# A transformer block with experts: order sums moved to accumulating transfers, a layer norm's statistics to ScalarE

## The reference, cut to what matters

```python
h = layernorm(x) * (1 + ca) + sa
x = x + ga * attention(h)        # x: (8, 1024, 256)
h = layernorm(x) * (1 + cb) + sb
x = x + gb * experts(h)

def attention(x):                # 16 heads of 16, orders n = 0..10, weight beta[n]
    q, k, v = x @ W_in.T, split into heads; xq, xk = clip(q / 4), clip(k / 4)
    Tq, Tk = chebyshev(xq), chebyshev(xk)
    num = sum_n Tq[n] * beta[n] * cumsum(Tk[n] * v)
    den = sum_n sum(Tq[n]) * beta[n] * cumsum(sum(Tk[n]))
    return (num / (den + 1e-7)) @ W_out.T

def experts(x):                  # 8 routed experts, 2 chosen, and one shared
    a = sqrt(softplus(x @ routing_W.T + bias)); top-2 of a give the weights
    return shared(x) + sum_e weight[e] * (silu(x @ W1[e] + b1[e]) @ W2[e] + b2[e])
```

## Time and profile before

| what | value |
|---|---|
| median of three runs | 1087.46 us (1085.91 to 1087.97) |
| the profiled execution | 1086.55 us |
| its span | 1084.9 us |
| PE busy | 948.9 us, 87% |
| DVE busy | 947.9 us, 87% |
| ACT busy | 472.5 us, 44% |
| POOL busy | 516.6 us, 48% |
| mean granted PE clock | 0.952 of full speed |

### The profile page before, as it was taken

The page is one execution under the profiler, slowest core; times in us unless marked ns, Lnnn a source line. Parts: engine busy times, 40 slices in busy tenths (PEclk is TensorE's granted clock), DMA queues, the critical chain, the costliest instruction groups (busy, mean ns, idle before and its releaser), DMA issues.

```text
span 1084.9 us, 15500 instructions
## 1 busy us (share of the span) xinstructions
PE 948.9 (87%) x4889; PEld 678.4 (63%) x4889; DVE 947.9 (87%) x1465; ACT 472.5 (44%) x702; POOL 516.6 (48%) x615
## 2 busy tenths in 40 slices
PE   3864749998998989999999999898999999889996
PEld 3643436675756666675757576675757576656774
DVE  1498989999999999999999999999999999999432
ACT  4334335372635445362635444362635445441431
POOL 2032646646645546536645546536645445454210
PEclk9876869999999999999999999999999999999999
DMA  8100001020202002020202011020202010020211
GB/s 270 45 1 20 20 0 50 1 59 1 69 1 59 1 9 60 0 58 0 69 0 58 0 16 53 0 58 0 69 0 39 0 24 25 1 39 1 44 21 20
DMA packets 31517, 34.18 MB, mean 32 GB/s; under 512 B 1299, under 2 KB 30430, under 8 KB 31462
## 3 DMA queue, kind: packets, MB, share of 16 engines
q1 hardware_dynamic: 21410, 22.72, 6.3%
q0 software_dynamic: 8448, 8.39, 5.9%
q10 hardware_dynamic: 1604, 2.46, 0.7%
HBM read 16.77 MB, written 16.79 MB: 31 GB/s over the span
## 4 chain that ended last, share of the span: by engine, by line
PE 32%; DVE 30%; issue 18%; POOL 11%; ACT 3%; DVEq 1%; POOLq 0%; ACTq 0%
PE ring L1257 13%; PE acc L1394 7%; DVE feat L945 7%; PE tr L1342 4%; PE tr L1310 4%; DVE feat L966 3%; POOL feat L625 2%; DVE hid L1094 2%; DVE feat L962 2%; DVE feat L1004 2%; DVE feat L1001 2%; POOL ms L357 1%; PE tr L1248 1%; DVE route L1083 1%; PE cfb L1368 1%
## 5 line engine op out<-in xcount | busy, mean ns | idle before, releaser
L784 ACT ACTIVATE hid<-ring,b1row 128x512 f32<-128x512 f32 x144 | 98.6, 685 | 163.5 <-PE ring L1257 163.5
L630 POOL TENSOR_TENSOR feat<-feat 128x1024 f32<-128x1024 f32 x32 | 75.6, 2364 | 197.7 <-DVE feat L962 152.8
L1394 PE MATMUL acc<-w,hid 128*128 128x256 f32 x640 | 156.6, 392 | 0.0
L1394 PEld LDWEIGHTS acc<-w,hid 128*128 128x128 f32 x640 | 117.1, 191 | 28.0 <-issue 14.5
L945 DVE TENSOR_TENSOR_SCAN feat<-zero,carry,feat 128x512 f32<-128x512 f32 x80 | 113.1, 1453 | 0.0
L945 DVE TENSOR_TENSOR_SCAN feat<-zero,feat 128x512 f32<-128x512 f32 x80 | 109.9, 1413 | 0.0
L1094 DVE TENSOR_TENSOR hid<-hid,cfb 128x512 f32<-128x512 f32 x128 | 86.2, 673 | 25.7 <-PE cfb L1368 25.3
L1257 PE MATMUL ring<-n2H,w1H 128*128 128x512 f32 x288 | 101.9, 436 | 0.0
L1257 PE MATMUL ring<-n1H,winH 128*128 128x512 f32 x192 | 67.3, 433 | 38.7 <-ACT hid L784 24.9
L742 ACT ACTIVATE feat<-ring,bqkv 128x512 f32<-128x512 f32 x96 | 65.7, 686 | 71.5 <-PE ring L1257 71.5
L382 ACT ACTIVATE ntok<-xin,ms 128x256 f32 (+1 forms) x64 | 33.2, 589 | 138.5 <-POOL ms L361 138.5
(11 more groups left out here) (169 smaller groups left out, 2238.7 us busy)
## 6 DMA issues: line engine op xcount, KB each, us to landing
xin<-in_L_attn_x SPq DMA_DIRECT2D x16, 512.0 KB, 5.5
out<-x SPq DMA_DIRECT2D x16, 512.0 KB, 4.5
out<-fin POOLq DMA_DIRECT2D x16, 512.0 KB, 6.2
gates<-gate_rows SPq DMA_DIRECT2D x16, 128.0 KB, 4.8
feat<-in_L_wmod SPq DMA_DIRECT2D x1, 1536.0 KB, 14.1
feat<-in_L_attn_W_in SPq DMA_DIRECT2D x1, 768.0 KB, 9.5
const<-in_constants ACTq DMA_DIRECT2D x1, 690.5 KB, 4.3
fin<-in_constants ACTq DMA_DIRECT2D x1, 512.0 KB, 5.2
```

The costliest lines, as they stand in the source:

```text
L630: g.tensor_tensor(f(W + 2 * n), f(W + 2 * n), f(W + 2 * n + 1), ALU.add).then_inc(added, 1)
L784: a.activation(hid[:, e % NG], ring[bank][:, :], ACT.Silu, bias=b1row[:, e:e + 1]).then_inc(ring_copied, 1)
L1394: last = mm(acc[t // 2][:, t % 2], x[:, t * P:(t + 1) * P], w[:, e // 2], start=False, stop=(e == E), skip_group_check=True)
```

## The change

- The second norm's statistics leave DVE. ACT takes the sum of each token with a Copy pass that also accumulates (`token_sums`), POOL makes minus the mean (`token_means`), ACT takes the sum of squared differences with a Square pass (`token_squares`, two halves), and POOL makes the scale and the shift with four operations (`inv_std_of_squares`). The passes' own output goes to an unused slot, `squared`, which is W+2.
- ACT's order: the sums stand before silu 2, the squares between the copies of k0, k1 and q0, `scale_even` behind `normalise_second`, `normalise_first` behind the high part of expert 6, the squares of the next chunk's keys between silu 6 and silu 7.
- `add_orders` becomes three accumulating transfers issued by POOL: W+1 to W, W+3 to W+4, then, when both have landed, W+4 to W. DVE's numerator keeps one add (W+2).
- DVE's order: the orders are scanned as 0, 1, 3, 4, 2; the scans of orders 3 and 4 stand right behind expert 3; the weighing of order 2, the first norm's statistics, the clips and the logit parts behind expert 4; the last numerator add before expert 8. The carry copies are merged from five to three.
- The softplus series is fitted anew with fewer terms: 10 operations instead of 13.

```diff
@@ -12,6 +12,7 @@
 K = 2
+LOG1P = (2.0000000076817583, 0.666663216413768, 0.40024595230747134, 0.2796515774481493, 0.2815777836368378)
...
@@ -148,6 +149,7 @@
         attn = feat[:, W + 1]
+        squared = feat[:, W + 2].rearrange("p h (a d) -> p (h a) d", a=NT // KD)
...
@@ -258,7 +263,7 @@
         ffn_gated = sem("ffn_gated")
-        NLOG, NSOFT, NCF, NSPLIT, NMV = 7, 13, 3, 7, 11
+        NLOG, NSOFT, NCF, NSPLIT, NMV = 7, 10, 3, 7, 11
@@ -373,6 +378,41 @@
+        def token_sums(act, i, p):
+
+            c = number(i, p)
+            for t in range(NT):
+                act.wait_ge(x1_ready, 2 * c + 1 + t // 2)
+                last = nc.scalar.activation(squared[:, t], x1[:, p, t], ACT.Copy, accum_out=ms[:, 1, 0, t:t + 1])
+            last.then_inc(sums_ready, 1)
+
+        def token_means(pool, i, p):
+
+            pool.wait_ge(sums_ready, number(i, p) + 1)
+            nc.gpsimd.tensor_tensor(ms[:, 1, 1], ms[:, 1, 0], k_("-1/D", NT), ALU.mult).then_inc(mean_ready, 1)
+
+        def token_squares(act, i, p, half):
+
+            act.wait_ge(mean_ready, number(i, p) + 1)
+            for t in (2 * half, 2 * half + 1):
+                last = nc.scalar.activation(squared[:, t], x1[:, p, t], ACT.Square, bias=ms[:, 1, 1, t:t + 1],
+                                            accum_out=ms[:, 1, 2, t:t + 1])
+            last.then_inc(squares_ready, 1)
+
+        def inv_std_of_squares(pool, i, p):
+
+            c = number(i, p)
+            at = 3 * c
+            t = lambda k: ms[:, 1, k]
+            pool.wait_ge(squares_ready, 2 * c + 2)
+            nc.gpsimd.tensor_tensor(t(3), t(2), k_("1/D", NT), ALU.mult).then_inc(var_steps, 1)
+            pool.wait_ge(var_steps, at + 1)
+            nc.gpsimd.tensor_tensor(t(4), t(3), k_("eps", NT), ALU.add).then_inc(var_steps, 1)
+            pool.wait_ge(var_steps, at + 2)
+            nc.gpsimd.tensor_tensor(t(9), t(4), k_("-half", NT), ALU.pow).then_inc(var_steps, 1)
+            pool.wait_ge(var_steps, at + 3)
+            nc.gpsimd.tensor_tensor(t(11), t(1), t(9), ALU.mult).then_inc(rstd_ready[1], 1)
+
...
@@ -621,13 +661,20 @@
                 pool.wait_ge(odd_ready, 4 * c + 2)
-                ge(pool, numerator, 2 * c)
+                ge(pool, numerator, c)
                 g.tensor_tensor(f(W + 4), f(KT5), f(V0), ALU.mult).then_inc(weighted5, 1)
             def add_orders(i, p, n):
-                pool.wait_ge(products, ND * number(i, p) + 2 * n + 2)
-                g.tensor_tensor(f(W + 2 * n), f(W + 2 * n), f(W + 2 * n + 1), ALU.add).then_inc(added, 1)
+                c = number(i, p)
+                if n < 2:
+                    pool.wait_ge(products, ND * c + 2 * n + 2)
+                else:
+                    pool.wait_ge(added[0], 16 * c + 16)
+                    pool.wait_ge(added[1], 16 * c + 16)
+                into, of = ((W, W + 1), (W + 4, W + 3), (W, W + 4))[n]
+                pool.sem_inc(sum_begun, 1)
+                g.dma_start(f(into), f(of), accum_op=ALU.add).then_inc(added[n], 16)
@@ -689,20 +736,22 @@
                 if st["second"]:
-                    inv_std(pool, 1, *later(i, p, -1))
+                    token_means(pool, *later(i, p, -1))
+                    inv_std_of_squares(pool, *later(i, p, -1))
                 if st["attn"]:
                     weigh_order_5(i, p)
                     if p == 0:
                         scale_wo(i)
                     add_orders(i, p, 0)
+                    add_orders(i, p, 1)
+                if st["second"]:
+                    exps(*later(i, p, -1))
+                if st["attn"]:
+                    add_orders(i, p, 2)
                 if st["norm"]:
                     inv_std(pool, 0, *later(i, p, 2))
                 if st["second"]:
-                    exps(*later(i, p, -1))
                     scores(*later(i, p, -1))
-                if st["attn"]:
-                    add_orders(i, p, 1)
-                if st["second"]:
@@ -750,8 +799,11 @@
                     act.wait_ge(clipped, 2 * c + q + 1)
+                    ge(act, summed, 2 * c - 1 + q)
                     if q == 0:
-                        ge(act, summed, 2 * c)
+                        ge(act, weighted, (ND - 1) * c)
+                        ge(act, weighted5, c)
+                    else:
@@ -830,13 +882,21 @@
                     highs(0, *nxt)
+                if second:
+                    token_sums(act, *prev)
                 silu(2)
-                if attn_:
-                    scale_even(i, p)
-                for half in HALVES[:4]:
-                    copy(half)
+                copy("k0")
+                if second:
+                    token_squares(act, *prev, 0)
+                copy("k1")
+                if second:
+                    token_squares(act, *prev, 1)
+                copy("q0")
+                copy("q1")
                 if second:
                     normalise_second(act, *prev)
+                if attn_:
+                    scale_even(i, p)
@@ -844,20 +904,22 @@
                     copy_logits(*prev)
-                if st["norm"]:
-                    normalise_first(act, *later(i, p, 2))
                 silu(5)
                 high(4)
                 copy("v0")
                 copy("v1")
                 silu(6)
+                if qkv:
+                    for which in range(3):
+                        square(*nxt, 0, which)
                 silu(7)
                 high(6)
+                if st["norm"]:
+                    normalise_first(act, *later(i, p, 2))
                 silu(8)
                 if qkv:
-                    for q in range(2):
-                        for which in range(3):
-                            square(*nxt, q, which)
+                    for which in range(3):
+                        square(*nxt, 1, which)
@@ -913,12 +975,15 @@
-            ORDERS = (0, 1, 3, 2, 4)
+            ORDERS = (0, 1, 3, 4, 2)
+
+            BY_WEIGHT = (0, 1, 3, 2)
+            NCARRY, CARRIED = 3, {0: 1, 1: 1, 3: 2, 4: 2, 2: 3}
             def weigh(i, p, j):
                 c = number(i, p)
-                n = ORDERS[j]
+                n = BY_WEIGHT[j]
@@ -929,6 +994,7 @@
                     dve.wait_ge(odd_ready, 4 * c + 1)
+                    ge(dve, squares_ready, 2 * c)
@@ -936,18 +1002,22 @@
                 if n < 4:
-                    dve.wait_ge(weighted, (ND - 1) * c + j + 1)
+                    dve.wait_ge(weighted, (ND - 1) * c + BY_WEIGHT.index(n) + 1)
                 else:
                     dve.wait_ge(weighted5, c + 1)
                 if p:
-                    dve.wait_ge(carried, ND * i + j + 1)
+                    dve.wait_ge(carried, NCARRY * i + CARRIED[n])
                 for h in range(KD):
                     last = v.tensor_tensor_scan(feat[:, W + n, h], zero[:, 0:1].to_broadcast([P, CT]), feat[:, W + n, h],
                                                 carry[:, n, h:h + 1] if p else 0.0, ALU.add, ALU.add)
                 last.then_inc(scanned, 1)
+
+            def carry_over(i, p, k):
+
                 if p == 0:
-                    dve.wait_ge(scanned, ND * c + j + 1)
-                    v.tensor_copy(carry[:, n], feat[:, W + n, :, CT - 1]).then_inc(carried, 1)
+                    at, n, j = ((0, 2, 1), (3, 2, 3), (2, 1, 4))[k]
+                    dve.wait_ge(scanned, ND * number(i, p) + j + 1)
+                    v.tensor_copy(carry[:, at:at + n], feat[:, W + at:W + at + n, :, CT - 1]).then_inc(carried, 1)
@@ -997,15 +1067,12 @@
                 dve.wait_ge(products, ND * c + ND)
-                dve.wait_ge(added, 2 * c + 1)
-                v.tensor_tensor(f(W), f(W), f(W + 4), ALU.add).then_inc(numerator, 1)
-                dve.wait_ge(numerator, 2 * c + 1)
-                dve.wait_ge(added, 2 * c + 2)
+                dve.wait_ge(added[2], 16 * c + 16)
                 v.tensor_tensor(f(W), f(W), f(W + 2), ALU.add).then_inc(numerator, 1)
             def divide(i, p):
                 c = number(i, p)
-                dve.wait_ge(numerator, 2 * c + 2)
+                dve.wait_ge(numerator, c + 1)
@@ -1060,18 +1127,16 @@
                 v.tensor_tensor(b(Z2), b(Z), b(Z), ALU.mult).then_inc(soft_steps, 1)
-                dve.wait_ge(soft_steps, at + 4)
-                v.tensor_scalar(b(PL), b(Z2), 2.0 / 15, 2.0 / 13, ALU.mult, ALU.add).then_inc(soft_steps, 1)
-                dve.wait_ge(soft_steps, at + 5)
-                v.tensor_tensor(b(PL), b(PL), b(Z2), ALU.mult).then_inc(soft_steps, 1)
-                for k, m in enumerate((11, 9, 7, 5, 3)):
-                    dve.wait_ge(soft_steps, at + 6 + k)
-                    v.scalar_tensor_tensor(out=b(PL), in0=b(PL), scalar=2.0 / m, in1=b(Z2),
+                v.scalar_tensor_tensor(out=b(PL), in0=b(Z), scalar=LOG1P[4], in1=b(Z),
+                                       op0=ALU.mult, op1=ALU.mult).then_inc(soft_steps, 1)
+                for k, m in enumerate((3, 2, 1)):
```

(58 more changed lines are left out.)

13 lines of the change are left out of this document (8 added, 5 removed).

## The result

| | before | changed |
|---|---|---|
| median | 1086.68 us, 4 runs | 1126.27 us, 4 runs (1125.12 to 1127.35) |
| ratio to before | | 1.0364, interval 1.0345 to 1.0383 |
| span of the profiled execution | 1084.9 us | 1123.3 us |

The account below looks back on a forecast made before the run. PE and DVE were both taken as critical early, DVE's run from expert 4 late. Thirteen steps at +0.8 (+10.4) and -4 at the edges gave +6.4 on 1086.55: 1093, adjusted to 1094; range 1066 to 1122.

Parts of the forecast that it names:

- what moves into the late stretch: DVE from expert 4 to the divide's end: 5.7 us in, one scan pair out, 24.5 us instead of 24.7.
- +0.8: Predicted growth of each of 13 full steps in us, from +0.9 in p=1 and +0.7 in p=0.
- The -4 of the edge steps: First two steps and the one before the last two, DVE-bound: two save 2 us each, together -4.
- the early stretch: Step up to expert 4: ScalarE passes and POOL's product delay `cfb` 4 to +32.45, expert 4 to +32.9 from +32.2.
- The 0.6 us for expert 8's weighing behind the last add: End of step: weighing after the numerator's last add makes PE start the out-projection at +57.9, after the divide at +57.3.
- Rival B: POOL's queue: transfers land late, at 9 us instead of 6.2, delaying scores and divide; 36 us more, 1130; chance 0.15.
- The 0.6 us a step that a clip might have laid on an issue: POOL's transfer issues: by the skill's rule a DVE clip could delay one, 0.6 us a step, 1102 in all.
- Rival D: Transfers slow DVE by traffic as POOL's adds do: at most 0.4 us of one weighing returns; no chance given.
- Rival C: ScalarE's summing is free: 0.49 us per pass, squares 0.4 us earlier, 5 us less, 1089; chance 0.10.
- the scan pair beside POOL's product: DVE before expert 2: scans held by POOL's product, 4.6 us, ending +21.7 instead of +19.1; 0.5 more in p=0.
- Step (e): DVE's late wait of 1.71 us behind normalise_first goes when that moves behind expert 6's high part.
- Rival A: Passes and contention hide, `cfb` 4 stays at +30.55: 22 us less, 1065, half gives 1076; chance 0.32, whole or part.

Follow-up runs that it names:

- Experiments 1 to 3: Weighing of order 2 moved: earlier in the changed kernel (experiment 1, experiment 2); later in the kernel before, 1134.48 us, ratio 1.0438.
- experiment 2: Changed kernel with the weighing of order 2 moved half way, behind expert 4's low part and ahead of the logit parts: 1070.72 us, ratio 0.9849.
- experiment 10, the second: On experiment 5's kernel, expert 8's weighing put ahead of the last numerator add: 1043.13 us, ratio 0.9601.
- experiment 7: On experiment 1's kernel, the three accumulating transfers replaced by three 128x1024 adds on POOL: 1104.00 us, ratio 1.0159.
- experiment 5: On experiment 1's kernel, the second norm's statistics back on DVE, without ScalarE's eight summing passes: 1043.61 us, ratio 0.9603.
- experiment 1: Changed kernel with DVE's weighing of order 2 moved from behind the denominator products to just before expert 4: 1054.85 us, ratio 0.9708.
- experiment 6: On experiment 1's kernel, the weighing of the fifth order moved from POOL to DVE, before expert 2: 1063.40 us, ratio 0.9791.
- experiment 4: Changed kernel with the weighing of order 2 moved forward to before expert 2: 1065.96 us, ratio 0.9806.

## Why the prediction was right or wrong

**The step that failed** is the one on what moves into the late stretch. It priced the weighing of order 2 at 1.22 us of DVE time and asked only when DVE gets to it; who waits for it was never asked. It is the last reader of `V0`, and it releases the copies of v0 and v1, with PE's ring behind them. That wait was not in the sum and not among the rivals: +5.0 us of PE, +1.3 at the low clock, in each of 13 steps; net of the waits and the low clock that the kernel before had, 3.0 us in the step shown. The row was there to see: v0's copy comes right behind silu 5 at +36.4, and the weighing was to end at about +41. Experiments 1 to 3 show it. All told the step grew by 3.3 us where +0.8 stood. The -4 of the edge steps came out at -4.8.

**A second error partly hid the first.** With the slot's wait nearly gone and the DVE work in place (experiment 2), 13 steps take 59.6 us each, 1.0 less than in the kernel before, where the sum had 0.8 more. So the rest of the sum was 1.9 us a step too slow, some 24 us, and 1094 came nearer to 1126 than its parts were. Its mis-sized terms are those of the early stretch below, 1.4 us up to expert 4, and 0.7 us of the late one. The 0.6 us for expert 8's weighing behind the last add was nearly nothing as well (experiment 10, the second).

**Rival B, late transfers: wrong.** They land after 4.5 to 4.8 us, earlier than any value I took, and the scores have 5.7 us of slack. 1126 lies near its 1130 for another reason. The 0.6 us a step that a clip might have laid on an issue didn't show either: the 48 issues take 0.85 to 1.07 us, but in the step shown none runs beside a clip. **Rival D: wrong in size.** The adds' price on DVE was read from the places they had; in the new order it is 3.7 us of DVE and 3.2 us of the step, 49 us in all (experiment 7). The transfers' side of the change was mis-sized for that reason alone, and the error did not enter the sum, since the change has them.

**The early stretch: right in sign, too slow.** bn_stats (the second norm's statistics) were worth nothing where they lay: DVE waits 0.74 before expert 0's low part (1.4 expected) and 2.06 before expert 2 (2.4). Expert 2's high part was ready at +19.7 to +20.2, not +21.2, `cfb` 4 at +31.1, not +32.45, expert 4 at +31.5, not +32.9. The mis-sized terms: a summing pass is an ACTIVATE and a read-out of 0.20 us, but they overlap, and four sums take 1.6 us (480.41 to 482.00), 0.40 each, two squares 0.98 us, 0.49 each; I took 0.6, and even Rival C's 0.49 for all eight was too much. By the formula of the Trainium skill, ScalarE: Activation LUTs, What ACT_TABLE_LOAD costs, such passes lie an estimated 0.31 and 0.40 us apart without a sum; against that the read-out would add 0.09 to each. And the scan pair beside POOL's product (the forecast's "order 2", which is n = 1) took 3.63 us in p=1 and 4.28 in p=0, not 4.6: POOL began its product 1.0 us before the scan (489.89 and 490.88) and held it only for what was left, and in p=0 `scale_wo` held the second scan. That the summing passes cost and not gain was right: 11 us, 0.9 a step (experiment 5).

**The late stretch: right but for the slot.** 24.5 us expected from expert 4 to the end of the divide; the changed kernel has 506.36 to 532.62, 26.26, of which 2.48 are waits for PE, so 23.8 of work. Step (e) gave 19.4 of 22 us by itself. Rival A's bound of 1065 fell: experiment 1 has the change's parts all but one place and runs in 1054.9. Its steps take 58.6 us on average where the bound has 60.65 - 1.35 = 59.3; the weighing that it puts ahead of expert 4 had been counted behind.

## What to carry to other kernels

When an operation is moved, ask first what it releases: for a slot of which there is only one, the last reader is a release, and a later last reader is a later producer, here with three engines in the chain (DVE, ScalarE, PE). Idle time of one engine is usable only if no other engine's work depends on it; here POOL's small operations on the critical path did, and a product of 1.2 us on an idle DVE cost 8 to 11 us. And price an operation that contends by what will stand beside it in the new order, not by what stands beside it today.

## What the runs showed of the hardware

- An accumulating transfer of 512 KB from on-chip memory to on-chip memory landed after 4.5 to 4.8 us and was issued in 0.91 us (median of 48), against 6.2 and 1.33 for the same bytes added to a tensor in memory. The four scans beside the first (499.95 in the changed kernel) took 4.80 us, 1.20 each, as undisturbed ones do.
- An ACTIVATE with a sum is followed by an ACTIVATION_READ_ACCUMULATOR of 0.20 us. The Copy passes, 0.41 us long, lie 0.40 apart with it. Passes without a sum overlap by 0.10 (`normalise_second`: 0.59 long, 0.49 apart), so the read-out costs an estimated 0.09 us.
- A POOL operation of 128x4 took 0.20 us beside an idle DVE, and 0.56 to 1.72 us beside 128x1024 products of two on-chip inputs on DVE (2.83 at 447.91 of experiment 5, beside two in a row); the ones read in experiment 6 end 0.06 us behind DVE's. A 128x1024 product on POOL took 2.36 us where it began before DVE's scan (463.27 in experiment 1), and 3.3 to 3.4 us where DVE's scan or product had begun first (468.30 in experiment 4, 474.99 in the kernel before).
- PE, after 4.96 us without work, restarted at the 1.2 GHz level (granted clock 0.53 from 516 to 519, 1.00 from 519 to 522). After a wait of 1.19 us it stayed at the full level (experiment 2, 1.00 from 552 to 555). After 1.79 us (501.93 of the kernel before) it ran the first pair in 0.73 and fell to 0.52 from 503.00 to 506.40, while after 1.78 us (623.53 of the same run) it stayed at 1.00: six of the twelve such waits of that kernel were followed by the lower level, and these runs don't show what decides.
